# Last expert chunk: down products among the up products, output rows shared by VectorE and ScalarE

## The reference

```python
x = _layernorm(x + attention(x))          # (4, 512, 512)
logits = x @ Wr + br;  probs = softmax(logits)
top_w, top_idx = top_k(probs, 1)
h = silu(x @ Wg[e]) * (x @ Wu[e])         # e = top_idx, 512 -> 2048
y = (h @ Wd[e]) * top_w                   # 2048 -> 512
out = _layernorm(x + y)                   # (v - mean) / sqrt(var + 1e-5), per token
```

## Time and profile before

| | us |
|---|---|
| median of three runs | 1309.82 |
| the profiled execution, whole | 1316.87 |
| its span (first to last record) | 1315.0 |
| PE busy in the span | 1190.7 (91%) |
| DVE busy | 800.3 (61%) |
| ACT busy | 556.9 (42%) |
| POOL busy | 310.7 (24%) |
| granted TensorE clock, mean | 0.95 of full speed |

### The profile page before, as it was taken

One profiled execution on the slowest core, in us unless ns is written; L12 is line 12 of the kernel. 1 busy time (PEld: TensorE's weight loads), 2 busy tenths in 40 slices (PEclk: granted clock), 3 DMA queues, 4 the chain that ended last, 5 costly groups with the idle time before them and its releaser, 6 DMA issues.

```text
span 1315.0 us, 27997 instructions
## 1 busy us (share of the span) xinstructions
PE 1190.7 (91%) x8697; PEld 1074.6 (82%) x8697; DVE 800.3 (61%) x1999; ACT 556.9 (42%) x1341; POOL 310.7 (24%) x458
## 2 busy tenths in 40 slices
PE   5888998999899988579999999999999999999983
PEld 4777887888788776578998899889989998899861
DVE  4667777676767765646556654655566546554675
ACT  3567765675666574043323332323233323232310
POOL 4200200020020020363113311331133113311347
PEclk9999999999999988589999999999999999999975
DMA  8222323232322240162232232122222322232112
GB/s 249 61 59 54 69 69 97 48 71 65 97 49 57 65 121 1 65 178 71 81 82 58 73 89 74 58 73 81 81 58 72 92 71 69 61 96 67 33 41 88
DMA packets 109639, 100.13 MB, mean 76 GB/s; under 512 B 12799, under 2 KB 81791, under 8 KB 109504
## 3 DMA queue, kind: packets, MB, share of 16 engines
q1 hardware_dynamic: 106464, 89.16, 24.9%
q0 software_dynamic: 3040, 9.18, 2.2%
HBM read 64.74 MB, written 9.18 MB: 56 GB/s over the span
## 4 chain that ended last, share of the span: by engine, by line
PE 70%; POOL 7%; DVE 7%; issue 5%; ACT 4%; DMA 3%; SPq 3%; ACTq 0%; POOLq 0%; DVEq 0%
PE bank L762 34%; PE bank L552 12%; PE bank L787 9%; PE bank L678 4%; POOL up_lo L1320 4%; PE bank L661 3%; PE bank L774 2%; SPq L460 2%; DMA up_raw<-in_Wu_dram 2%; PE bank L650 2%; POOL out_dram L1368 2%; DVE scores L1047 1%; PE bank L638 1%; ACT probs L858 1%; DMA q_stack<-qk_hi 1%
## 5 line engine op out<-in xcount | busy, mean ns | idle before, releaser
L762 PE MATMUL bank<-up_hi,xsT_hi 128*128 x1216 | 357.1, 294 | 9.5 <-POOL up_lo L1320 7.7
L762 PE MATMUL bank<-up_hi,xsT_lo 128*128 x1216 | 345.0, 284 | 0.0
L762 PE MATMUL bank<-up_lo,xsT_hi 128*128 x1216 | 344.9, 284 | 0.0
L1320 POOL TENSOR_TENSOR up_lo<-up_raw,up_hi 128x256 fp32r<-128x256 f32 x241 | 169.7, 740 | 487.0 <-ACT up_hi L890 486.8
L1191 DVE SCALAR_TENSOR_TENSOR h_tok<-bank,row_weight,silu 128x128 f32<-128x128 f32 x304 | 93.4, 347 | 303.0 <-ACT silu L948 303.0
L762 PEld LDWEIGHTS bank<-up_hi,xsT_hi 128*128 128x128 f32 x1216 | 233.7, 192 | 15.8 <-issue 15.8
L762 PEld LDWEIGHTS bank<-up_hi,xsT_lo 128*128 128x128 f32 x1216 | 234.3, 193 | 0.0
L762 PEld LDWEIGHTS bank<-up_lo,xsT_hi 128*128 128x128 f32 x1216 | 234.0, 192 | 0.0
L948 ACT ACTIVATE silu<-bank 128x256 f32<-128x256 f32 (+1 forms) x160 | 59.6, 372 | 384.4 <-PE bank L762 384.4
L1208 DVE TENSOR_TENSOR y<-bank,y 128x512 f32<-128x512 f32 x304 | 205.0, 688 | 0.4
L858 ACT ACTIVATE probs<-scores,neg_max 128x512 f32<-128x512 f32 (+3 forms) x256 | 136.5, 557 | 72.2 <-DVE neg_max L1047 71.6
(11 more groups left out here) (155 smaller groups left out, 2124.5 us busy)
## 6 DMA issues: line engine op xcount, KB each, us to landing
up_raw<-in_Wg_dram SPq DMA_DIRECT2D x64, 256.0 KB, 3.1
up_raw<-in_Wu_dram SPq DMA_DIRECT2D x64, 256.0 KB, 4.0
down_raw<-in_Wd_dram SPq DMA_DIRECT2D x64, 256.0 KB, 2.7
k_stack<-qk_hi SPq DMA_DIRECT2D x128, 64.0 KB, 2.0
q_stack<-qk_hi SPq DMA_DIRECT2D x128, 64.0 KB, 2.0
x_tok<-in_x_dram SPq DMA_DIRECT2D x4, 1024.0 KB, 5.8
k_stack<-qk_lo SPq DMA_DIRECT2D x64, 64.0 KB, 2.0
q_stack<-qk_lo SPq DMA_DIRECT2D x64, 64.0 KB, 2.0
```

What stands on the lines that cost most here:

```text
L762: mm = pe.matmul(bank[:, n * 2 * P:(n + 1) * 2 * P], a[:, s, k, :], up_w[w][k][:, :, :].rearrange("p a f -> p (a f)")[:, bass.ds(at, 2 * P ...
L1320: pool.tensor_tensor(up_w[1][k][:, e, :], up_raw[:, idx % NUPS, k, :, :].rearrange("p g f -> p (g f)"), up_w[0][k][:, e, :].bitcast(F32), ...
```

## The change

The list of the last chunk is rewritten. Pairs whose hidden values are ready are multiplied down and finished while the up products of later pairs still run. `DOWN_WITH` says which: in the step of up pair 4 also pair 0, with 5 pair 1, with 6 pairs 2 and 3, with 7 pairs 4 and 5, with 8 pair 6, with 9 pair 7; pairs 8 and 9 come last.

- The last two steps of a pair (mean and variance, normalising) are shared: the even slot by VectorE as before, the odd slot by ScalarE. For the odd slot VectorE's add also makes the sum of the row (`tensor_tensor_reduce` with `accum_out`); ScalarE makes minus the mean, then a Square with that as bias and the sum of the squares as second output (the variance), and later the row as Identity with a scale and a shift per row.
- GpSimd makes the inverse deviations of both slots of a pair with one add and one power of two columns, and does all deviations of a step's pairs first, then all their stores.
- The rows are normalised in place in `y`; the four row buffers and the waits on them are gone.

```diff
+DOWN_WITH = {4: (0,), 5: (1,), 6: (2, 3), 7: (4, 5), 8: (6,), 9: (7,)}
+DOWN_AFTER = (8, 9)
# tensor
+            for pr in range(NPAIR):
+                up_pair(NC - 1, pr)
+                if pr >= 1:
+                    transpose_pair(NC - 1, pr - 1)
+                for done_pr in DOWN_WITH.get(pr, ()):
+                    for s in PAIRS[done_pr]:
+                        down_slot(NC - 1, s)
+            transpose_pair(NC - 1, NPAIR - 1)
+            for pr in DOWN_AFTER:
+                for s in PAIRS[pr]:
+                    down_slot(NC - 1, s)
# scalar
+            def final_squares(pr):
+                if len(PAIRS[pr]) == 2:
+                    s = PAIRS[pr][1]
+                    act.wait_ge(s_y, (NC - 1) * NS + s + 1)
+                    act.activation(y_mean[:, pr, 0:1], y_sum[:, pr:pr + 1], ACT.Copy, scale=-1.0 / D).then_inc(s_fmean, 1)
+                    act.activation(y_mean[:, pr, 1:2], y_sum[:, pr:pr + 1], ACT.Copy, scale=-D ** -1.5).then_inc(s_fmean, 1)
+                    act.wait_ge(s_fmean, 2 * pr + 2)
+                    act.activation(squares[:, :], y[:, s, :], ACT.Square, scale=D ** -0.5, bias=y_mean[:, pr, 1:2],
+                                   accum_out=y_mom[:, pr, 2:3]).then_inc(s_fsq, 1)
+            def final_row(pr):
+                if len(PAIRS[pr]) == 2:
+                    s = PAIRS[pr][1]
+                    act.wait_ge(s_frstd, pr + 1)
+                    act.activation(y_shift[:, pr:pr + 1], y_mean[:, pr, 0:1], ACT.Copy,
+                                   scale=y_rstd[:, pr, 1:2]).then_inc(s_fshift, 1)
+                    act.wait_ge(s_fshift, pr + 1)
+                    act.activation(y[:, s, :], y[:, s, :], ACT.Identity, scale=y_rstd[:, pr, 1:2],
+                                   bias=y_shift[:, pr:pr + 1]).then_inc(s_odd, 1)
...
+                    if c == NC - 1:
+                        for done_pr in DOWN_WITH.get(pr - 1, ()):
+                            final_squares(done_pr)
                     gate_pair(c, pr)
                     if pr >= 1:
                         transposed_pair(c, pr - 1)
                     if pr < NE:
                         split_down(c, pr)
+                    if c == NC - 1:
+                        for done_pr in DOWN_WITH.get(pr - 1, ()):
+                            final_row(done_pr)
...
+            transposed_pair(NC - 1, NPAIR - 1)
+            for pr in DOWN_WITH[NPAIR - 1]:
+                final_squares(pr)
+            for pr in DOWN_WITH[NPAIR - 1]:
+                final_row(pr)
+            for pr in DOWN_AFTER:
+                final_squares(pr)
+            for pr in DOWN_AFTER:
+                final_row(pr)
# vector
-            def final_moments(s):
...
+            def final_pair(pr):
+                for s in PAIRS[pr]:
+                    if s % 2 == 0:
+                        add_down(c, s)
+                    else:
+                        dve.tensor_tensor_reduce(out=y[:, s, :], in0=banks[D_BANKS[idx % 3]][:, :], in1=y[:, s, :],
+                                                 scale=1.0, scalar=0.0, op0=ALU.add, op1=ALU.add,
+                                                 accum_out=y_sum[:, pr:pr + 1]).then_inc(s_y, 1)
+                s = PAIRS[pr][0]
+                dve.bn_stats(stats[:, pr % 2, :], y[:, s, :]).then_inc(s_fst, 1)
+                dve.bn_aggr(y_mom[:, pr, 0:2], stats[:, pr % 2, :]).then_inc(s_fmv, 1)
+            def final_row(pr):
+                s = PAIRS[pr][0]
+                dve.wait_ge(s_frstd, pr + 1)
+                dve.tensor_scalar(y[:, s, :], y[:, s, :], y_mom[:, pr, 0:1], y_rstd[:, pr, 0:1],
+                                  ALU.subtract, ALU.mult).then_inc(s_even, 1)
...
+                    if c == NC - 1:
+                        for done_pr in DOWN_WITH.get(pr - 1, ()):
+                            final_row(done_pr)
+                        for done_pr in DOWN_WITH.get(pr, ()):
+                            final_pair(done_pr)
...
+            transposed_pair(NC - 1, NPAIR - 1)
+            for pr in DOWN_AFTER:
+                final_pair(pr)
+                for done_pr in DOWN_WITH[NPAIR - 1] if pr == DOWN_AFTER[0] else ():
+                    final_row(done_pr)
+            for pr in DOWN_AFTER:
+                final_row(pr)
# gpsimd
+            def final_deviation(pr):
+                m = len(PAIRS[pr])
+                pool.wait_ge(s_fmv, pr + 1)
+                if m == 2:
+                    pool.wait_ge(s_fsq, pr + 1)
+                pool.tensor_scalar(y_var[:, pr, 0:m], y_mom[:, pr, 1:1 + m], EPS, None, ALU.add).then_inc(s_fvar, 1)
+                pool.wait_ge(s_fvar, pr + 1)
+                pool.tensor_tensor(y_rstd[:, pr, 0:m], y_var[:, pr, 0:m], mhalf[:, 0:m], ALU.pow).then_inc(s_frstd, 1)
...
+            for together in [DOWN_WITH[pr] for pr in range(NE, NPAIR)] + [DOWN_AFTER]:
+                for pr in together:
+                    final_deviation(pr)
+                for pr in together:
+                    for s in PAIRS[pr]:
+                        final_store(s)
+            pool.wait_ge(s_out, 16 * NS)
```

More of the change, by code:

```diff
@@ L282, in build @@
         rstd = keep.put("rstd", [P, 2, 2], F32)
-        mhalf = keep.put("mhalf", [P, 1], F32)
+        mhalf = keep.put("mhalf", [P, 2], F32)
+        y_sum = keep.put("y_sum", [P, NPAIR], F32)
+        y_mean = keep.put("y_mean", [P, NPAIR, 2], F32)
+        y_mom = keep.put("y_mom", [P, NPAIR, 3], F32)
+        y_var = keep.put("y_var", [P, NPAIR, 2], F32)
+        y_rstd = keep.put("y_rstd", [P, NPAIR, 2], F32)
+        y_shift = keep.put("y_shift", [P, NPAIR], F32)
         top = nc._sbuf_addr_for_side("right") // 32 * 32 - 4 * 2 * QT * D
@@ L288, in build @@
         up_raw = Map(raw_at).put("up_raw", [P, NUPS, KT, 2, P], F32)
-        final = Map(raw_at)
-        out_rows_sb = [final.put(f"out_row{n}", [P, D], F32) for n in range(LN_BUFS)]
+        squares = Map(raw_at).put("squares", [P, D], F32)
         p1 = Map(keep.at)
@@ L389, in build @@
         s_down, s_y = semaphore("down_products"), semaphore("y_added")
[L390 removed]
+        s_fst, s_fmv, s_fsq = semaphore("final_stats"), semaphore("final_moments"), semaphore("final_squares")
+        s_fmean, s_fshift = semaphore("final_mean"), semaphore("final_shift")
+        s_even, s_odd = semaphore("even_rows_done"), semaphore("odd_rows_done")
         s_fvar, s_frstd = semaphore("final_variance"), semaphore("final_rstd")
[L392 removed]
+        s_out = semaphore("out_written")
         def done(*job):
@@ L790, in down_slot @@
                 mm.then_inc(s_down, 1)
-            for c in range(NC):
+            for c in range(NC - 1):
                 for pr in range(NPAIR):
@@ L967, in scalar @@
                         split_down(c, pr)
-                for s in range(NS):
-                    if c + 1 < NC and s % 3 == 0 and s // 3 < NE:
+                    if c == NC - 1:
+                        for done_pr in DOWN_WITH.get(pr - 1, ()):
+                            final_row(done_pr)
+                for s in range(NS if c + 1 < NC else 0):
+                    if s % 3 == 0 and s // 3 < NE:
                         split_up(c + 1, s // 3)
@@ L1208, in add_down @@
                 dve.tensor_tensor(y[:, s, :], banks[D_BANKS[idx % 3]][:, :], y[:, s, :], ALU.add).then_inc(s_y, 1)
-            def final_moments(s):
[L1211 to L1224, removed]
+            def final_pair(pr):
+                c = NC - 1
+                for s in PAIRS[pr]:
+                    idx = c * NS + s
+                    if s % 2 == 0:
+                        add_down(c, s)
+                    else:
+                        dve.wait_ge(s_down, idx + 1)
+                        dve.wait_ge(s_y, idx - NS + 1)
+                        dve.tensor_tensor_reduce(out=y[:, s, :], in0=banks[D_BANKS[idx % 3]][:, :], in1=y[:, s, :],
+                                                 scale=1.0, scalar=0.0, op0=ALU.add, op1=ALU.add,
+                                                 accum_out=y_sum[:, pr:pr + 1]).then_inc(s_y, 1)
+                s = PAIRS[pr][0]
+                dve.wait_ge(s_y, c * NS + s + 1)
+                dve.bn_stats(stats[:, pr % 2, :], y[:, s, :]).then_inc(s_fst, 1)
+                dve.wait_ge(s_fst, pr + 1)
+                dve.bn_aggr(y_mom[:, pr, 0:2], stats[:, pr % 2, :]).then_inc(s_fmv, 1)
[4 more added lines that the diff above has]
+                                  ALU.subtract, ALU.mult).then_inc(s_even, 1)
             for c in range(NC):
@@ L1235, in vector @@
                         split_down(c, pr)
-                for s in range(NS):
-                    if c + 1 < NC and s == 0:
+                    if c == NC - 1:
[3 more added lines that the diff above has]
+                            final_pair(done_pr)
+                for s in range(NS if c + 1 < NC else 0):
+                    if s == 0:
                         dve.wait_ge(s_uphi, (c + 1) * NE * KT + 1)
@@ L1358, in gpsimd @@
```

(11 more changed lines are left out.)

19 lines of the change are left out of this document (5 added, 14 removed).

## The result

The changed kernel takes 1293.61 to 1299.14 us in four runs, median 1294.69 us; the ratio to the kernel before is 0.9874, 95% interval 0.985 to 0.9898. Timed once more (r8), it was 0.9893 (0.9868 to 0.9919). So it is 1.1 to 1.3% faster by the two ratios, 14 to 17 us. Forecast: 1292.3 us, range 1290 to 1298.5.

A forecast was written before the change was run, and what follows sets the result against it. GpSimd's list bounds the end: start 1250.5 + deviations 9.0 + stores 24.7 + 1.1 + waits 7.2 = 1292.5 against 1310.2, 17.7 less. Off the median 1309.8: 1292.1, or 1292.3 with the power's columns not quite free; range 1290 to 1298.5.

The forecast's parts named there:

- GpSimd's list bounds the end: Last chunk, kernel before: GpSimd's adds, powers and stores run without waiting for data, 2.47 us a period, and set the end.
- New start, 1250.5: GpSimd's first deviation in the last chunk starts at 1250.5 us, 12.8 us earlier than before.
- Ten deviations at 0.90: GpSimd's add and power for each pair's inverse deviations, at the one-column price: 9.0 us in all.
- 19 stores at 1.30, three with 0.36 more: GpSimd's stores: 1.00 plus 0.30 gap each, 24.7 us; three beside another even row being made add 1.1.
- The rival of 1.35 us stores: Stores keep 1.35 us, or VectorE's or ScalarE's new operations cost their upper bounds: 1297 us; chance 0.13.
- Waits of 7.2 us: Waits in GpSimd's list, steps 4 to 9, for Squares, rows and deviations: 7.2 us in all.
- waits for Squares of pairs 1, 2, 3: GpSimd's waits for ScalarE's Squares of slots 3, 5 and 7, steps 5 and 6: 0.2, 0.2 and 1.4 us.
- step 9: GpSimd waits 0.2 us for the Square, then 1.5 for row 14 behind slots 16 and 17's adds and statistics.
- Gain 17.7 us: GpSimd's last store ends at 1292.5 us in place of 1310.2.
- TensorE's clock: Rival: TensorE's clock falls to half early, among interleaved products: 1295 us, or 1309.8 with no change; chance 0.05, 0.01 for the latter.
- the slower rival: ScalarE's Square pulls in another activation table, 11 switches: 1301 us, or 1321 and slower; chance 0.03, slower 0.01 to 0.02.
- The rule of the shared port: Even rows (VectorE's) cost GpSimd 0.4 us each where they fall on a store's start, ScalarE's rows never.

The follow-up runs named there:

- r8: The changed kernel, unedited, timed and profiled again; ratio to before 0.9893, tail (start of last chunk's first up product to end of last store) 63.2 us.
- r3: Kernel before, with the 19 rows normalised by ScalarE in place of VectorE's tensor_scalar; ratio 0.9981, tail 75.9 us against 79.0.
- r7: Changed kernel without GpSimd's ten adds of eps (1e-5 under the root); one run, tail 61.8 us.
- r1: Kernel before with only the change's order: down products among up products, every slot finished as before, nothing shared; ratio 0.9883, tail 64.5 us.
- r5: Changed kernel with a step's rows placed ahead of the next pair's silu and product on VectorE and ScalarE; ratio 0.9906, tail 66.0 us.
- r2: Kernel before with only the sharing: down products after all up products, finished by pairs as in the change; ratio 0.9948, tail 70.9 us.
- r4: Changed kernel with guarded variance and inverse deviation in one tile in place of two; one run, tail 63.1 us.
- r9: The kernel of r7 (no eps adds) profiled again; one run, tail 61.6 us.
- r6: Changed kernel with down products two pairs at a time, with up pairs 4, 5, 6 and 8, then the last two; ratio 0.9883, tail 60.2 us.
- r10: The kernel of r6 again, beside the change in the same call; ratio 0.9899, tail 59.9 us.

## Why the prediction was right

- *GpSimd's list bounds the end, from 1263.25 to 1310.2.* Right for the kernel before: r3 shortens the stores, and the tail follows by 3.1 us. For the changed kernel it holds only in part (r7).
- *New start, 1250.5, that is 19.3 us into the chunk.* Measured 19.32. VectorE's summing add 0.68 + 0.08, ScalarE's two tiny ones and Square with its accumulator read 1.15 from the first start to the end of the read: 0.2 less than the 0.4 + 0.95 that I had set for them, since they overlap. The handing on from engine to engine, 0.12 and 0.15, took that up again, so the hit to 0.1 us is in part luck.
- *Ten deviations at 0.90.* 1.04 each; I had kept the second column's price as an open bound of up to 0.32 and it was 0.15, so 1.5 us more of work in all.
- *19 stores at 1.30, three with 0.36 more.* Stores 0.97 to 1.08 plus 0.30, and only two longer ones (1.28, 1.17): right on the cause, 0.6 us too dear in all. The rival of 1.35 us stores fell. My reading of the stores of before had one slip: 1.10 us was the second store, not the third, and the other short ones took 1.09 and 1.17. r3 has 1.09 with no row of VectorE at all, so this is the price of a store behind GpSimd's own arithmetic, which I had read as a row in mid-store.
- *Waits of 7.2 us.* Their sum was right (7.0) and their make-up was not. I took a store to start 0.30 us after its row. Where GpSimd stands waiting for the row it takes 0.8: VectorE's row 12 ended at 1273.14 and its store started at 1273.95, row 4 at 1258.2 and 1259.01, and so (0.80 to 0.89) in all the six groups whose first store waited. That is 3 us which my list lacks.

```profile
1272.59 0.55 DVE L1292 TENSOR_SCALAR y<-y,y_mom,y_rstd 128x512 f32<-128x512 f32 x1 [2.62 <-POOL y_rstd L1443]
```

  The waits for Squares of pairs 1, 2, 3 (0.2, 0.2, 1.4) shrank instead to 0.3 in all, because GpSimd came later to them. For step 9 I had 1.5 behind the adds of slots 16 and 17, measured 1.1 with the same 0.8 in it. Errors of about 3 us each way cancelled, which is luck; the list came to 42.9 us against 42.0 predicted.
- *Gain 17.7 us.* 16.8 in the profiled pair; 15.8 with the late increments of the second profile. The whole time, 1294.69 us, lies 2.4 us above the forecast.
- *TensorE's clock.* It fell some 47 us into the chunk, behind the last up products, so none of the work that the rival priced ran at half speed. The rival wasn't far: in r1 and r5 the granted clock was 0.60 and 0.57 in stretches that hold interleaved up products, after waits of TensorE of 2.1 and 3.3 us. In r1 this cost nothing that its tail shows; VectorE was its bound there.
- *Table loads.* One for the silu, as before: the Square needed none, and the slower rival fell. The Trainium skill (ScalarE: Activation LUTs, "What ACT_TABLE_LOAD costs") puts a switch to a different set at 2.66 us; no run here has such a switch in the tail, so none shows that figure.
- *The rule of the shared port*, by which VectorE's `tensor_scalar` shuts GpSimd out (the Trainium skill, SBUF — State Buffer, "SBUF: two separate sides"). The runs agree where the row starts first: 1.35 us under VectorE's row, 1.09 and less beside ScalarE's (r3). No run shows the port itself.
- What the prediction did not ask is what each half of the change is worth without the other. It priced GpSimd's work at 34.8 us in place of 46.9, so 12.1 us less, and let the waits eat 7.2 of them; with the order already in place the sharing brings 1.3 to 2.3 (r1), and without it 8.1 (r2).

## What to carry to other kernels

Before paying for a cheaper tail, move its start: taking the finished work among products that still run gave 14.5 of 16.8 us here by reordering the work of four engines; the sharing between two engines gave the rest, too little for the whole times to tell. Once the start is early, the engine that was the bound waits for its feed in part of the steps, and cutting its work (the eps adds) returned under half of what was cut. And an order that puts a short wait ahead of another engine's feed (rows first) cost more than the wait it shortened, and TensorE's clock fell beside it (r5, one profile).

## What I had not expected

- **Who is stretched depends on who starts first.** A `tensor_scalar` that begins just before a store makes the store 1.35 us. One that begins 0.53 us into a store becomes 0.78 us instead of 0.55 in ten of eleven cases, and the store stays 1.09 (r1). But one that begins right at the start of a store stretches neither, as in the kernel before, where the row starts 0.04 us into the store (another, 0.22 us in, likewise); why the place within the store matters stays open:

```profile
1270.72 1.09 POOL L1368 DMA_INDIRECT out_dram<-out_row,out_token  x1 [0.19 <-issue]
...
1270.76 0.55 DVE L1223 TENSOR_SCALAR out_row<-y,mv,rstd 128x512 f32<-128x512 f32 x1
```

- **A store that GpSimd waits for starts 0.8 us after its row**, against 0.30 us behind another store.
- **Late increments of TensorE.** A matmul that ends a group of products raises a semaphore, the increment, on which the next engine waits. In r8 the last product of up pair 8 is recorded from 1265.18 to 1265.46 us; the silu, with ScalarE idle, starts at 1266.89, when the down products of slot 12 are done and the last of slot 13 is running. ScalarE and TensorE of r8:

```profile
1258.51 0.39 ACT L969 ACTIVATE silu<-bank 128x256 f32<-128x256 f32 x1 [0.49 <-PE bank L772]
1266.89 0.39 ACT L969 ACTIVATE silu<-bank 128x256 f32<-128x256 f32 x1 [1.71 <-PE bank L772]
```

```profile
1265.18 0.28 PE L772 MATMUL bank<-up_lo,xsT_hi 128*128 x1
1265.30 0.38 PE L784 MATMUL bank<-ident,h_tok 128*128 128x128 f32 x2
...
1266.66 0.39 PE L797 MATMUL bank<-down_lo,hT_hi 128*128 x1
```

In this profile the increments of up pair 8 and of slots 12 and 13 are recorded within 0.2 us of each other, though the products lie 0.7 us apart. For the other up pairs of r8 the increment is recorded 0.01 to 0.02 us after the recorded end of the product, for pair 8 it is 1.4 us. The first profile of the same program doesn't have it, nor does r5; r4, r7 and r9 have it at pair 8 (1.4 to 1.5 us), r6 and r10 at pairs 6 and 7 (1.4 to 1.6). The tail with it is 1 us longer (63.2 against 62.2). The ends of matmuls in a profile are modelled, so the products themselves may have ended later than recorded; what is late, and why, stays open.
